# Layer 1 attention in a twelve-layer kernel: exponentials by head from PSUM, normalised before the turn, values as stationary operand

## What is computed

```python
q = einsum('bxy,iyk->bxik', x, Wq).reshape(h, b, t, hs)      # 16 heads, 64 wide; k and v alike
wei = einsum('hbqd,hbkd->hbqk', q, k) * hs ** (-0.5)
wei = where(causal, wei, -inf)
wei = softmax(wei, axis=-1)
out = einsum('hbqk,hbkd->hbqd', wei, v)
out = out.reshape(b, t, h * hs) @ proj_w.T + proj_b
```

## Time and profile before

| what | us |
|---|---|
| median of three runs | 1354.98 (1354.49 to 1362.57) |
| the profiled execution's own time | 1347.55 |
| its span (first to last instruction) | 1345.8 |
| PE busy in the span | 1187.5 (88%) |
| DVE, ACT, POOL busy | 689.3, 522.4, 437.5 (51%, 39%, 33%) |
| the stage of the change, first to next stage's first instruction | 228.2 to 376.8, or 148.6 |

### The profile page before, as it was taken

How to read it: one execution, slowest core, us unless ns; L and a number is a source line. 1 busy time by engine, 2 the same in 40 slices (tenths; PEclk the granted TensorE clock), 3 DMA queues, 4 the chain that set the end, 5 groups by cost and what they waited for, 6 DMA issues and landing times. The chain is left out here.

```text
span 1345.8 us, 24227 instructions
## 1 busy us (share of the span) xinstructions
PE 1187.5 (88%) x9574; PEld 851.9 (63%) x9574; DVE 689.3 (51%) x2134; ACT 522.4 (39%) x1173; POOL 437.5 (33%) x519
## 2 busy tenths in 40 slices
PE   6999988999958775898789899999989999978997
PEld 5877766788833343466466566795657775556575
DVE  5545543333569535576377366727842125755512
ACT  5534242444346432345345442323433333433332
POOL 7959530000055422674467240003000001031414
PEclk9999988999987578899899987999989998989899
DMA  5000231422075000000000000000021010000412
GB/s 167 1 4 1 88 117 47 127 64 64 1 236 132 1 1 34 0 1 1 0 2 0 1 9 1 2 4 1 2 86 48 32 31 1 1 4 1 147 45 52
DMA packets 51633, 52.42 MB, mean 39 GB/s; under 512 B 19553, under 2 KB 42337, under 8 KB 50497
## 3 DMA queue, kind: packets, MB, share of 16 engines
q1 hardware_dynamic: 50496, 48.78, 11.5%
q0 software_dynamic: 1024, 2.10, 0.7%
HBM read 43.66 MB, written 7.21 MB: 38 GB/s over the span
## 5 line engine op out<-in xcount | busy, mean ns | idle before, releaser
L625 ACT ACTIVATE scratch<-bank 128x512 f32<-128x512 f32 x96 | 52.4, 594 | 80.5 <-PE bank L524 80.5
L447 POOL TENSOR_TENSOR ln_rstd<-ln_ve,ln_half 128x4 f32<-128x4 f32 x28 | 28.7, 1026 | 155.2 <-DVE ln_ve L426 155.1
L584 DVE TENSOR_REDUCE scratch<-bank 128x4 f32<-128x512 f32 x96 | 61.7, 682 | 25.0 <-PE bank L2510 13.7
L2764 POOL TENSOR_TENSOR scratch<-scratch 128x16 f32<-128x16 f32 x16 | 51.7, 3231 | 50.3 <-DVE scratch L3106 50.3
L1126 ACT ACTIVATE scratch<-bank 128x512 f32<-128x512 f32 x64 | 38.2, 597 | 67.6 <-PE bank L1085 67.6
L1095 PEld LDWEIGHTS bank<-scratch 128*128 128x128 f32 x512 | 59.5, 192 | 7.2 <-issue 7.2
L1145 DVE SCALAR_TENSOR_TENSOR x_res<-bank,scratch,x_res 128x128 f32<-128x128 f32 x64 | 18.0, 344 | 87.8 <-PE bank L1095 87.8
L590 DVE TENSOR_TENSOR scratch<-bank,scratch 128x512 f32<-128x512 f32 x96 | 61.3, 679 | 0.0
L1085 PE MATMUL bank<-xnT,scratch 128*128 128x512 f32 x128 | 59.2, 608 | 0.5 <-DMA scratch<-e_l_ffn_w 0.5
L1095 PE MATMUL bank<-scratch 128*128 128x128 f32 x512 | 59.6, 275 | 0.0
L524 PEld LDWEIGHTS bank<-ident,scratch 128*128 128x128 f32 x384 | 43.1, 144 | 22.2 <-DVE scratch L590 16.8
(11 more groups left out here) (569 smaller groups left out, 2979.9 us busy)
## 6 DMA issues: line engine op xcount, KB each, us to landing
scratch<-conv_kernels SPq DMA_DIRECT2D x8, 1024.0 KB, 11.2
scratch<-e_l_ffn_w SPq DMA_DIRECT2D x20, 256.0 KB, 3.0
scratch<-e_l_ffn_w SPq DMA_DIRECT2D x4, 1024.0 KB, 14.6
values<-scratch SPq DMA_DIRECT2D x8, 512.0 KB, 2.6
scratch<-values SPq DMA_DIRECT2D x8, 512.0 KB, 4.4
weights<-w_l_ffn SPq DMA_DIRECT2D x1, 3698.0 KB, 11.6
scratch<-e_l_ffn_w SPq DMA_DIRECT2D x4, 768.0 KB, 9.3
weights<-w_l_attn SPq DMA_DIRECT2D x1, 2560.5 KB, 8.7
```

The lines of the kernel that those rows point to most:

```text
L584: self.nc.vector.tensor_reduce(self.top[:, n % 4, :], self.by_head(self.core.ps[n % 4][:, :]), AX_X, ALU.max, negate=True).then_inc(self.t ...
L625: self.nc.scalar.activation(self.prob_of(n), self.by_head(self.core.ps[4 + n % 2][:, :]), ACT.Exp, scale=scale) \
L2764: nc.gpsimd.tensor_tensor(rn, ss, power, ALU.pow).then_inc(rooted.sem, rooted.up())
```

## The change

The softmax of a step goes another way round. Scores stay in PSUM; ACT takes the exponential of each head by itself from there (8 instructions a step, with the maximum as bias and the row sum as a second output). DVE inverts the sums, POOL scales the probabilities, PE turns them over, DVE copies them to SBUF. The values become the stationary operand (64 columns) and the turned probabilities the moving one (128 columns), so the product comes out transposed and ready for the output projection. The transposes of the outputs, the column of ones, the subtraction and the scaling of outputs on DVE go. One of three projection fills is emptied by DVE, the other two by ACT. Scores are made two steps ahead and stand after the projections in a turn, and projections start a turn earlier. The diff, cut to its core:

```diff
-    TURNS = range(-5, STEPS + 2)
+    TURNS = range(-6, STEPS + 1)
...
+    by_dve = lambda name: name[0] == "in" and name[2] % PER_TURN == 1
 @block.gpsimd
+            for n in TURNS:
+                if 0 <= n + 1 < STEPS:
+                    for i in range(2):
+                        part = prob[:, (n + 1) % 2, 4 * i:4 * i + 4, :]
+                        pool.wait_ge(inverse.sem, inverse.at(2 * (n + 1) + i))
+                        nc.gpsimd.tensor_tensor(part, part, inv[:, (n + 1) % 2, 4 * i:4 * i + 4].unsqueeze(2)
+                                                .broadcast_to([P, 4, P]), ALU.mult).then_inc(scaled.sem, scaled.up())
 @block.tensor
-                        pe.wait_ge(shifted.sem, shifted.at(2 * n + i))
+                        pe.wait_ge(scaled.sem, scaled.at(2 * n + i))
                         if n > 0:
-                            pe.wait_ge(exped.sem, exped.at(2 * (n - 1) + i))
+                            pe.wait_ge(copied.sem, copied.at(2 * (n - 1) + i))
...
                     for i in range(2):
+                        if n + 2 > 0:
+                            pe.wait_ge(exped.sem, exped.at(2 * (n + 1) + i))
                         nc.tensor.matmul(by_head(ps[S_BANKS[i]][:, :]), core.ident_bf[:, :],
...
                     for i in range(2):
-                        if n > 0:
-                            pe.wait_ge(normed.sem, normed.at(2 * (n - 1) + i))
-                        pe.wait_ge(exped.sem, exped.at(2 * n + i))
-                        for j in range(4):
-                            t = nc.tensor.matmul(ps[O_BANKS[i]][:, j * (K + 1):(j + 1) * (K + 1)], prob[:, 4 * i + j, :],
-                                                 vaug[:, b % 4, 8 * i + n % 2 * 4 + j, :], start=True, stop=True)
-                        t.then_inc(valued.sem, valued.up())
+                        pe.wait_ge(copied.sem, copied.at(2 * n + i))
+                    for j in range(4):
+                        for i in range(2):
+                            t = nc.tensor.matmul(ps[O_BANKS[n % 2]][rows(i), j * P:(j + 1) * P],
+                                                 values[:, b % 4, 8 * i + n % 2 * 4 + j, :],
+                                                 probT[:, i, j * P:(j + 1) * P], start=True, stop=True)
+                    t.then_inc(valued.sem, valued.up())
 @block.scalar
             for n in TURNS:
+                if 0 <= n + 1 < STEPS:
+                    r = (n + 1) % 2
+                    for i in range(2):
+                        act.wait_ge(tops.sem, tops.at(2 * (n + 1) + i))
+                        if n >= 1:
+                            act.wait_ge(turned.sem, turned.at(2 * (n - 1) + i))
+                        for j in range(4):
+                            a = nc.scalar.activation(prob[:, r, 4 * i + j, :], ps[S_BANKS[i]][:, j * P:(j + 1) * P],
+                                                     ACT.Exp, bias=top[:, i, j:j + 1],
+                                                     accum_out=total[:, r, 4 * i + j:4 * i + j + 1])
+                        a.then_inc(exped.sem, exped.up())
...
+                for name in projections(n):
+                    if not by_dve(("in", *name)):
+                        empty(*name)
                 if 0 <= n < STEPS:
+                    act.wait_ge(valued.sem, valued.at(n))
+                    at = (n // 2 % 2 * 8 + n % 2 * 4) * 8
                     nc.scalar.copy(oT[:, :, at:at + 32].rearrange("p i (j t) -> p i j t", t=8),
+                                   ps[O_BANKS[n % 2]][:, :].rearrange("p (j t i) -> p i j t", j=4, t=8)) \
+                        .then_inc(outs.sem, outs.up())
```

More of the change, by code:

```diff
@@ L1872, in layer_l1_attn, with placed @@
         order += [] if finished(n) is None else [("yT", finished(n), i) for i in range(2)]
[L1873 removed]
+        order += [("in", u, m) for u, m in projections(n)]
         order += [] if finished(n) is None else [("y", finished(n))]
     place = {name: f for f, name in enumerate(order)}
+    by_dve = lambda name: name[0] == "in" and name[2] % PER_TURN == 1
+    emptied_by = {}
+    for count, names in ((emptied, [n for n in order if not by_dve(n)]), (emptied_dve, [n for n in order if by_dve(n)])):
+        emptied_by.update((name, (count.sem, count.at(n))) for n, name in enumerate(names))
+    def placed(u, m, src):
+        dst, first, scale = (qT, 4 * (m - 4), K ** -0.5) if m < 8 else (kT, 4 * (m - 8), 1.0)
+        return (dst[:, u % 2, :, :].rearrange("p s (t i) -> p s t i", i=H)[:, :, :, first:first + 4],
+                src[:, :].rearrange("p (i s t) -> p s t i", i=4, t=8), scale)
     with nc.Block(tag, no_gpsimd_drain=True) as block:
@@ L1881, in _ @@
             for b in range(B):
-                sp.wait_ge(emptied.sem, emptied.at(place["in", b // 2, b % 2 * 2 + 1]))
+                for m in range(2):
+                    sp.wait_ge(*emptied_by["in", b // 2, b % 2 * 2 + m])
                 if b >= 2:
@@ L1957, in _ @@
                                 t.then_inc(scores.sem, scores.up())
-                if finished(n) is not None:
-                    pe.wait_ge(emptied.sem, emptied.at(place["o", 4 * finished(n) + 3]))
-                    outs = [bank(), bank()]
-                    for h in range(H):
-                        for i in range(2):
-                            t = nc.tensor.matmul(outs[i][:, 0:P], wp[rows(i), h, :], oT[rows(i), h, :],
-                                                 start=(h == 0), stop=(h == H - 1))
-                            if h == H - 1:
-                                t.then_inc(filled.sem, filled.up())
-                for u, m in projections(n):
-                    if u == 2 and m == 0:
-                        pe.wait_ge(x_out.sem, x_out.at(1))
-                    project(u, m)
-                if n == -5:
-                    norm.pe(pe, 1, O_BANKS[1])
                 if 0 <= n < STEPS:
@@ L2001, in _, with bank @@
         def _(act):
-            fills = itertools.count()
-            def bank():
-                f = next(fills)
-                act.wait_ge(filled.sem, filled.at(f))
-                return ps[F_BANKS[f % 2]]
+            def bank(*name):
+                act.wait_ge(filled.sem, filled.at(place[name]))
+                return ps[F_BANKS[place[name] % 2]]
             def empty(u, m):
-                src = bank()
+                src = bank("in", u, m)
                 if m < 4:
                     b = 2 * u + m // 2
-                    if b >= 2 and m % 2 == 0:
+                    if b >= 2:
                         act.wait_ge(stored.sem, stored.at(b - 2, 16))
@@ L2027, in _ @@
             for n in TURNS:
-                if 0 <= n < STEPS:
-                    for i in range(2):
-                        act.wait_ge(turned.sem, turned.at(2 * n + i))
-                        nc.scalar.activation(prob[:, 4 * i:4 * i + 4, :], by_head(ps[T_BANKS[i]][:, :]), ACT.Exp) \
-                            .then_inc(exped.sem, exped.up())
-                if finished(n) is not None:
-                    for i in range(2):
-                        nc.scalar.activation(yT[:, :, rows(i)], tokens(bank()[:, 0:P]), ACT.Identity, bias=bp) \
-                            .then_inc(emptied.sem, emptied.up())
@@ new lines, in _ @@
+                u = finished(n)
+                if u is not None:
+                    for i in range(2):
+                        nc.scalar.activation(yT[:, :, rows(i)], tokens(bank("yT", u, i)[:, 0:P]), ACT.Identity, bias=bp) \
+                            .then_inc(emptied.sem, emptied.up())
+                for name in projections(n):
+                    if not by_dve(("in", *name)):
+                        empty(*name)
+                if 0 <= n < STEPS:
+                    act.wait_ge(valued.sem, valued.at(n))
+                    at = (n // 2 % 2 * 8 + n % 2 * 4) * 8
+                    nc.scalar.copy(oT[:, :, at:at + 32].rearrange("p i (j t) -> p i j t", t=8),
+                                   ps[O_BANKS[n % 2]][:, :].rearrange("p (j t i) -> p i j t", j=4, t=8)) \
+                        .then_inc(outs.sem, outs.up())
@@ L2048, in _ @@
+                if u is not None:
+                    src = bank("y", u)
+                    if u > 0:
+                        act.wait_ge(added.sem, added.at(u - 1))
                     nc.scalar.copy(y.rearrange("p b d -> p (b d)"), src[:, 0:2 * D]).then_inc(emptied.sem, emptied.up())
```

145 lines of the change are left out of this document (77 added, 68 removed).

## The result

| | median us | runs | ratio to before, 95% interval |
|---|---|---|---|
| before | 1357.31 | 20, 1353.71 to 1365.21 | |
| after | 1368.91 | 20, 1359.46 to 1375.91 | 1.0072, 1.0056 to 1.0088 |

The kernel after is 0.7% slower, 9.8 us of 1357 by the ratio (7.6 to 12). In the profiled executions the stage took 158.5 us (229.6 to 388.1) against 148.6, which is 9.9 more. The two agree, but not too much should be read into that: the profiled execution of the kernel after, with 1375.91, was the slowest of its 20. The two spans differ by more, 1374.1 against 1345.8; where that comes from is told at the end of the experiments.

A forecast was written before the change was run, and what follows sets the result against it. PE bounds the stage before; after, PE's saved 1.34 us a step becomes a wait for ACT. Stage +3.0 and one clock fall +2.5 make +5.5 us on a median of 1354.98: 1360.5, range 1343 to 1376.

The forecast's parts named there:

- likeliest case: Whole kernel: PE's savings turn into a wait for ACT, +5.5 us; chance 0.60, and 0.72 for any result within 1%.
- full turn: Mid-stage turn with three fills and no output projection: 7.6 us between starts of the mask, against 7.58 before.
- turns -1 and 0: First turns of the stage, without values: maxima, exponentials, emptying, fill and scores take 6.7 us.
- last turns: Turns without projections: the second mask matmul waits for all eight exponentials, so 5.9 us against 4.77 before.
- stage without clock: Whole changed stage, before any loss of PE clock: 3.0 us longer.
- clock: PE's clock in the stage: one fall to half speed, 2.5 us added to the sum.
- The loop: Mid-stage chain of scores, values, copy of outputs, exponentials, emptying, third fill, scores: about 7.6 us a turn.
- one such fall: A drop to half clock in the last turns, doubling values 0.94 and mask and scores 1.35: taken as 2.5 us.
- The first, PE sets the pace: Turns follow PE's own work at 6.24 us, not ACT's queue: -9 or -16.5 us; chance 0.12.
- the rival's smaller form: PE sets the pace in seven ordinary turns and turns -1 and 0 only: -9 us, 1346.
- The second, exponentials or values at full price: Exponentials do not overlap (4.74 for eight), +29 us, or values still cost 1.83, +17 us; chance 0.10.
- The third, a falling clock in full turns: PE's 1.4 us rest before fill three lowers its clock, 3.5 us more per turn hit; chance 0.18.

The follow-up runs named there:

- doubled values: The kernel after with each values matmul on PE made twice, result unchanged: ratio to before 1.0150, full turn 8.53 to 8.60 us.
- doubled transposes: The kernel after with each of a step's eight transposes on PE made twice, result unchanged: ratio to before 1.0061, full turn 7.64 to 7.72 us.
- the moved emptying: The kernel after, but from the second unit on DVE empties a turn's first fill and ACT the second and third: ratio to before 1.0000.
- filling PE's waits: The kernel after with unused identity matmuls in PE's waits of turns -1 and 0 and at the end: ratio to before 1.0041.
- short exponentials: The kernel after, but one 512-column exponential per half replaces four, with the first head's maximum and one common row sum: ratio to before 0.9927.

## Why the prediction came out as it did

I said +5.5 us, 1360.5, with a range of 1343 to 1376, and within 1% as likeliest. Measured were +9.8 (7.6 to 12) and 1368.9. The likeliest case and its mechanism hold; the sum was 4.3 us short. The medians lie 8.4 apart, since the 20 runs of the kernel before also had a median 2.3 us above the three that I had, and the two medians differ by 1.8 more than the ratio says.

| step of the prediction | foretold | measured |
|---|---|---|
| eight exponentials | 2.75 | 2.75 |
| values, on PE, to the next start | 0.94 | 1.02 to 1.03 |
| full turn | 7.6 | 7.65 to 7.73 |
| PE's wait before fill three | 1.4 | 1.06 to 1.23 |
| turn with output projection, the one after | 10.3, 8.0 | 10.78, 8.00 |
| turns -1 and 0 | 6.7 | 6.9 to 7.0 (and 1.4 of clock) |
| last turns | 5.9 | 6.0 |
| start of the stage to first mask, against before | +3.5 | +3.9 |
| end of the scores of step 15 to the last output projection | 9.2 | 9.98, of it 0.9 of clock |
| stage without clock | +3.0 | +5.6 |
| clock | +2.5 | +4.3 |

**The loop.** The full turn, worked out by laying ACT's and PE's lists beside each other, came out within 0.1 us, and the doubled values, doubled transposes and the moved emptying show that it is this loop. Of the 0.15 us by which values and turned step took longer than in my list (see below), only 0.04 reached the third fill: it started 5.07 after the scores' end, for 5.03. That a whole 1.2 us a turn on PE could be taken away for nothing, with ACT half idle, was readable beforehand.

**What failed first: the size of the falls.** "I take one such fall into the sum, 2.5 us": the profile had two, 1.4 in turn -1 and 2.9 at the end, and filling PE's waits gave 4.2 us (1 to 7) back in the runs. I had priced a fall at what PE has on a loop of the last turns. At the end, though, the values and a whole output projection stand in a row with nothing beside them, so every half-speed matmul is bare. The kernel before took the same projection at full clock, after PE had been busy 6.57 of 8.2 us; in the kernel after PE had been busy 4.40 of the 8 us ahead of it. That alone does not decide it: with short exponentials PE had been busy 5.12 of 8 us, with nearly the same waits, and the projection took 3.84. What decides where a fall comes stays open, and that the sum needed one fall or two was a guess. The clock of 1.00 did not need a PE that "never rests" either: it held in full turns with a wait of 1.06 to 1.23 us in each.

**What failed second: "values 0.94" and "turned 0.87".** I subtracted 1.34 a turn from PE. PE's own turn, seen with short exponentials, is only 1.2 shorter: values and turned step take 2.0 us together in the timeline (309.54 to 311.50), where I had 1.81. In full turns most of that lies in the wait (which is why the wait was 1.2 and not 1.4). In the turns with an output projection it is bare: its matmuls began 2.05 us after the scores instead of 1.81, and the gap behind them and the fills added 0.2. Two such turns make 1.0; five full turns make 0.5, turns -1 and 0 0.4, the start 0.4, the last turns 0.3: together the missing 2.6.

**PE's busy time** in the stage, "down by some 25 us", fell by 10.2. The sum in the prediction itself gives 21.4 and not 25. The 1.34 that was 1.2 takes 2.4 off, and matmuls at half clock, which count as busy for longer, some 4.3 more. For the last 4.5 I have no account; busy time of overlapping matmuls was a poor thing to forecast.

**Rivals.** The first, PE sets the pace, did not come because of ACT's queue, as argued. With short exponentials PE does set the pace in full turns, and the kernel is 9.9 us faster than before (the stage 11.3). That is near the 9 of the rival's smaller form, but not the same thing: its last turns took 4.5 us and not the 5.9 of that form, and its clock did not fall in the stage. The second, exponentials or values at full price, is excluded by the rows (2.75 and 1.03). The third, a falling clock in full turns, did not come in any profile: the clock was 1.00 from 290 to 335 with PE busy 90%. But the falls around it cost 4.3 us, more than one such turn (3.5). POOL was hidden in full turns and bare at the end, as said; its multiplication took 1.04 us, all 32 times. "The rows agree" on POOL set it against a copy or maximum on DVE (0.69), which have one input; no run has the multiplication on DVE.

## What to carry to other kernels

When work is taken off the engine that bounds a stage, the gain is what the next loop of waits leaves of it. Write down the lists of all engines for one turn and look for a short instruction that frees a buffer but is queued behind long ones: here a 0.6 us emptying behind 2.75 us of exponentials cost 1.1 us in each turn, and giving it to another engine was one line. Then look at the ends of the stage, where little hides a hand-over: here start and end grew by 9.2 us, of which 2.8 was work moved there from the middle, and the middle by 0.7. A long piece of PE's work that stands alone there, such as the last output projection, is also where a fallen clock cost most.

## What was not expected

- A profiled execution can be off by 12 us in a stage that has nothing to do with the change: the last stage took 98 us once and 110 to 112 else.
- With turn -1 and the end filled, a turn near 346 fell, which had not in the kernel after. Whether the filling moved a fall there is not shown: five other variants, four of them without any filling, have one near the end too.
- An exponential of 128x128 from PSUM with a bias from SBUF: 0.25 us one after the other, while each is listed with 0.36 to 0.42 in the kernel after; with its accumulator read 0.34.
